# Graph network kernel on one core: neighbour counts moved into the later edge passes, and a first pass that takes stored and directly gathered tiles two and two

## The chip, the cores and the metric

The kernel runs on one core of a Trainium2 chip. The metric is the device time of one execution in microseconds (us). The engines are named as in the profile: PE (TensorE; PEld its weight loads), DVE (VectorE), ACT (ScalarE), POOL (GpSimd) and SP (SyncE). A "q" behind a name is that engine's instruction queue.

## The reference

There are 6250 nodes with 128 features and 106,250 directed edges, sorted by destination (`src`, `dst`). Four residual blocks follow each other, each with `x = layernorm(x + block(x))`:

- block 0, an attention layer: for each edge `s = leaky_relu(el[src] + er[dst])`, a softmax over the edges of one destination, and the weighted sum of the rows `(x @ W)[src]`;
- block 1, a message network: edge features (106,250 x 128) summed by source, then linear and softplus layers on the nodes;
- block 2, three attention layers of the same kind as block 0, with an edge term from three edge attributes, and batch norm in between;
- block 3, five layers `h + sum of h[src] over the edges of dst`, each followed by two linear layers and batch norms.

Block 3 needs, five times, the product of the features with the 6250 x 6250 matrix of edge counts ("how often does edge (i, j) occur"). This matrix is built once.

## The kernel before

**Tiles and steps.** Nodes lie in 49 blocks of 128 (`NB`). Edges lie in 208 tiles of 512 (`T`, `TE`; `W` = 4 columns of 128 edges). A tile whose edges end in two destination blocks is handled twice, so an edge pass has `K` = 256 steps for 208 tiles. The rows `(x @ W)[src]` are fetched by indirect DMAs of POOL from `gat_rows` in DRAM, 128 rows of 520 bytes each, four for a tile.

**The edge pass** `gat_edges` runs four times: once for block 0 (`streamed=True`), three times in a loop for block 2. In a later pass `fetch` gathers every tile into a `ring` of 16 tiles (L1204); SP waits until a slot is free and passes it on as `room`, and tells ACT over `tiles` which tiles have landed. `pipeline` writes the program of each engine by hand: 16 steps (`U`) in a loop body, before which the engine loads all registers of these steps. In a step, PE spreads the scores of step n (L1315), multiplies the weights of step n-7 with the ring's rows (L1324) and transposes the weights of step n-5 (L1331). DVE adds mask and scores (L1372), adds a product to the state (L1382), applies the slope (L1387), fetches scores (L1339), takes the maximum (L1345) and makes a mask (L1354). ACT adds a bias (L1402), loads a row for the mask by DMA (L1424), copies transposed weights out of PSUM (L1410), takes negatives (L1414) and the exponential (L1419). Four banks of PSUM hold spread scores, two the transposed weights, two the products.

**The streamed pass.** The gathered rows of block 0 don't depend on the stages before its pass. `gather_first_layer(begin, end)` is called by four earlier stages; POOL gathers tiles into five buffers (L1221) and stores each to `gathered` in DRAM itself (L1213). The pass then only loads them, by SP (L1240): 32 tiles are gathered in `positions`, 46 in `source_sums`, 12 in `adjacency_steps`, 118 in `adjacency`.

**The stages before the first pass**, each ended by a barrier of all engines (`end_phase`):

- `positions` finds for each edge its place in the order by source block. It runs over the source blocks twice in 26 chunks of 2048 edges, a count first, then comparison, scan, product and 32 small matmuls a chunk.
- `sort_rows` scatters the edge features to these places (POOL, L697) and counts rare edges.
- `source_sums` loads the sorted rows (SP, L1450) and sums them by source: comparison on DVE (L1483), matmuls (L1474), addition (L1494).
- `adjacency_steps` makes the tables for the count. The matrix is cut into 49 x 13 windows of 128 x 504 (`NKEY` = 637); a step adds the edges of one sorted tile to one window. POOL gathers twelve tables (L850).
- `adjacency` makes the counts in 1472 steps: DVE makes two tiles of ones and zeros (L1531, L1534), PE multiplies them into one of 8 banks (L1524), ACT copies pairs of windows out (L1568), clears the banks (L1570) and stores the pair (L1556).

The three functions of block 3 (`aggregate`, `second_layer`, `relu_norm`) read the matrix by SP (L1658).

## Time and profile before

| what | us |
|---|---|
| median of three runs | 8978.68 (8977.43 to 8986.32) |
| the profiled execution | 8993.16 |
| its span, first to last instruction | 8991.8 |
| mean granted clock of PE | 0.798 of full |
| busy: PE / DVE / ACT / POOL | 5567.6 / 4739.3 / 4511.6 / 4381.9 |

The profile is of one execution; its groups and windows below refer to its span. "Busy" adds up the durations of instructions, which on PE and ACT overlap a little; the distance between two starts is the better measure of what an instruction costs in a queue. The stages follow each other in time, so one reads a stage by giving the view its stretch: `positions` 177 to 487, `sort_rows` to 1552, `source_sums` to 1943, `adjacency_steps` to 2043, `adjacency` to 2746, the streamed pass 2770 to 3448, the later passes from 3690, 4840 and 5988, block 3 from 7170.

### The profile page before, as it was taken

Reading aid. Unit: us, or ns where it says so; the run is one execution under the profiler, and the core shown is the slowest. Engines: PE = TensorE matmul, PEld = TensorE weight load, DVE = VectorE, ACT = ScalarE, POOL = GpSimd, SP = SyncE. Lnnn points to the kernel's source line nnn. Section 1 sums busy time; section 2 is a strip of 40 time slices with the busy share of each in tenths; the row PEclk is TensorE's granted clock in tenths of the full one; section 3 lists DMA queues with packets and bytes.
Section 4 is the critical chain, followed back from the end, with each engine's and each line's share of the span. In section 5 each row is a group of like instructions: output and inputs, shape, how many; then the busy total and the mean of one; then the engine's idle time right before and its main releaser. Section 6 shows DMA issues by size and latency. Waiting matters only on the chain. (4 is left out here: it accounts for less than half of the span.)

```text
span 8991.8 us, 135316 instructions
## 1 busy us (share of the span) xinstructions
PE 5567.6 (62%) x30230; PEld 4477.6 (50%) x30231; DVE 4739.3 (53%) x12204; ACT 4511.6 (50%) x8872; POOL 4381.9 (49%) x4415
## 2 busy tenths in 40 slices
PE   1621111756776886466665666656666498998986
PEld 1610001742225774355554555645555487776865
DVE  3820000559997877555554555555555645445455
ACT  1038886008996774444444444444444444444344
POOL 1877777737771000477774777747777300000000
PEclk8555555878888998787886888778888799999998
DMA  3433334855665441233332333323333286676764
GB/s 102 120 101 105 107 105 111 233 136 183 211 211 160 135 131 46 65 84 85 84 84 70 85 84 84 85 69 84 84 84 84 57 264 199 217 251 199 252 212 154
DMA packets 724312, 1173.04 MB, mean 130 GB/s; under 512 B 118807, under 2 KB 546470, under 8 KB 723608
## 3 DMA queue, kind: packets, MB, share of 16 engines
q1 hardware_dynamic: 366644, 612.04, 22.0%
q0 software_dynamic: 150784, 336.22, 15.6%
q10 hardware_dynamic: 206628, 221.92, 8.7%
q8 instruction: 94, 1.54, 0.1%
q14 instruction: 162, 1.33, 0.0%
HBM read 955.51 MB, written 216.73 MB: 130 GB/s over the span
## 5 line engine op out<-in xcount | busy, mean ns | idle before, releaser
L1204 POOL DMA_INDIRECT ring<-gat_rows,src_idx x2496 | 2417.8, 969 | 1004.4 <-issue 1001.3
L1324 PE MATMUL ps<-ring,xT_b 128*128 x8192 | 1410.3, 325 | 1236.1 <-ACT xT_b L1410 1230.7
L1324 PEld LDWEIGHTS ps<-ring,xT_b 128*128 128x128 f32 x8192 | 1219.0, 228 | 1448.8 <-issue 1446.9
L1402 ACT ACTIVATE xT_a<-xT_a,state 128x514 f32<-128x514 f32 x1024 | 740.1, 723 | 1824.0 <-SPq L1176 1293.5
L1814 PE MATMUL ps<-wide,features 128*128 128x504 f32 (+1 forms) x6370 | 1438.8, 384 | 18.2 <-DVE features L1714 16.2
L1814 PEld LDWEIGHTS ps<-wide,features 128*128 128x128 f32 x6370 | 1156.8, 189 | 252.3 <-DVE wide L1682 17.4
L1372 DVE CUSTOM_DVE_ANT_0 xT_a<-ps,mask,xT_a 128x512 f32<-128x512 f32 x1024 | 767.0, 749 | 607.5 <-PE ps L1315 488.8
L697 POOL DMA_INDIRECT by_src<-ring,state x832 | 803.4, 966 | 255.9 <-issue 253.0
L1054 POOL TENSOR_TENSOR x_nodes<-x_nodes,last_state 128x1280 f32<-128x1280 f32 x3 | 9.9, 3312 | 1792.2 <-SPq L227 1792.2
L1315 PE MATMUL ps<-ident,s_col 128*128 128x128 f32 x4096 | 747.0, 315 | 187.5 <-DVE s_col L1339 122.5
L1419 ACT ACTIVATE xT_b<-xT_a,neg 128x514 f32<-128x514 f32 x1024 | 741.6, 724 | 33.1
L1331 PE MATMUL ps<-ident,xT_b 128*128 128x128 f32 x4096 | 751.8, 316 | 4.8 <-ACT xT_b L1419 4.8
L1387 DVE SCALAR_TENSOR_TENSOR xT_a<-xT_a 128x514 f32<-128x514 f32 x1024 | 704.1, 688 | 0.0
L1339 DVE TENSOR_TENSOR s_col<-ring,al_cols 128x4 f32 (+1 forms) x1036 | 166.5, 161 | 1019.5 <-ACTq L1400 980.5
L1680 DVE CAST wide<-xT_a 128x2016 fp32r<-128x2016 f16 (+27 forms) x440 | 410.8, 953 | 541.3 <-PE ps L1814 515.2
L1315 PEld LDWEIGHTS ps<-ident,s_col 128*128 128x128 f32 x4096 | 589.3, 164 | 211.3 <-DVE s_col L1339 128.0
L664 PE MATMUL ps<-xT_a 128*128 128x50 bf16 x832 | 184.4, 222 | 805.7 <-ACT xT_a L653 805.7
L1694 ACT ACTIVATE wide<-xT_a 128x1008 fp32r<-128x1008 f16 (+3 forms) x385 | 372.3, 978 | 605.0 <-PE ps L1814 594.2
L1221 POOL DMA_INDIRECT dl_all<-gat_rows,src_idx x484 | 571.5, 1181 | 147.6 <-issue 147.0
L1331 PEld LDWEIGHTS ps<-ident,xT_b 128*128 128x128 f32 x4096 | 598.9, 167 | 7.7 <-ACT xT_b L1419 7.7
L1410 ACT ACTIVATE xT_b<-ps 128x512 f32<-128x512 f32 x1024 | 595.6, 582 | 9.5 <-PE ps L1331 9.2
L664 PEld LDWEIGHTS ps<-xT_a 128*128 128x128 bf16 x832 | 87.1, 105 | 903.2 <-ACT xT_a L653 850.3
(383 smaller groups left out, 8761.4 us busy)
## 6 DMA issues: line engine op xcount, KB each, us to landing
xT_a<-adjacency SPq DMA_DIRECT2D x245, 756.0 KB
dl_all<-dloc_rows ACTq DMA_DIRECT2D x1052, 128.0 KB, 3.1
xT_b<-adjacency SPq DMA_DIRECT2D x150, 812.0 KB
xT_a<-adjacency SPq DMA_DIRECT2D x95, 812.0 KB
adjacency<-xT_b ACTq DMA_DIRECT2D x294, 252.0 KB
ring<-by_src SPq DMA_DIRECT2D x52, 1040.0 KB
ring<-gathered SPq DMA_DIRECT2D x208, 260.0 KB
ring<-in_edge_attr SPq DMA_DIRECT2D x103, 512.0 KB
```

What stands on the lines that cost most here:

```text
L697: pool.indirect_dma_start(by_src[:, :], bass.IndirectOffsetOnAxis(pos[:, g * L1U + u:g * L1U + u + 1], 0), ring[:, b * group + u * RC:b * ...
L1204: pool.indirect_dma_start(ring[:, o:o + RC], None, table[:, :], bass.IndirectOffsetOnAxis(src_idx[:, t * W + u:t * W + u + 1], 0)).then_in ...
L1221: pool.indirect_dma_start(held[h][:, u * RC:(u + 1) * RC], None, gat_rows[:, :], bass.IndirectOffsetOnAxis(src_idx[:, i:i + 1], 0)).then_i ...
L1315: m = pe.transpose(bank(BS + u % 4)[:, w * P:(w + 1) * P], s_col[u % 4][:, w:w + 1].to_broadcast([P, P]), ident[:, :])
L1324: m = pe.matmul(bank(BO + v % 2, R), pw[v % 4][:, w * P:(w + 1) * P], ring[:, w * RC:][:, bass.ds(look(SLOT, u - 7), R)], start=w == 0, st ...
L1331: m = pe.transpose(bank(BP + v % 2)[:, w * P:(w + 1) * P], pt[v % 8][:, w * P:(w + 1) * P], ident[:, :])
L1372: dve.tensor_tensor_reduce(out=m[:, 0:TE], in0=bank(BS + u % 4, TE), in1=mask[u % 4][:, :], scale=1.0, scalar=m[:, TE + 1:TE + 2], op0=ALU ...
L1387: dve.scalar_tensor_tensor(w, w, 0.2, w, ALU.mult, ALU.max).then_inc(q["leaky"], 1)
L1402: act.activation(um[u % 4], sm[u % 8], ACT.Identity, bias=S[:, ER:][:, bass.ds(look(BC, u), 1)]).then_inc(q["act_a"], 1)
L1410: act.activation(pw[v % 4], bank(BP + v % 2, TE), ACT.Copy).then_inc(q["pw_ready"], 1)
L1419: act.activation(pt[v % 8], um[v % 4], ACT.Exp, bias=neg[v % 4][:, :]).then_inc(q["weights"], 1)
L1814: m = pe.matmul(bank_of(w), H2[:, (i * 2 + x) * D:(i * 2 + x + 1) * D], wide[n % 2][:, o:o + width_of(w)], start=i == 0 and x == 0, stop=F ...
```

## The change

- **`adjacency` is gone.** Its counting is spread over the three later passes. The windows' steps are laid out for 2 streams x 3 passes x 256 steps = 1536. In each step of a later pass, for each of two streams, DVE makes the two tiles (`make_nodes`), PE multiplies the stream's last evicted window by the identity or by zeros (`carry`) and adds the new tile's product (`add_counts`), ACT copies the window out of PSUM (`evict_counts`) and in the next step stores it (`store_counts`): to its place in `counts` if the window ends there, to a row for waste otherwise. PE loads 16 registers each 8 steps, ACT 4 each 2 steps. Spread scores have two banks instead of four in these passes; the other two hold the two streams' windows. A window that both streams share is joined after the loop (four serial steps, three of them DMAs).
- **The tables** go to DRAM at the end of `adjacency_steps` (`of_steps`, `step_rows`) and each pass loads its third (`load_steps`).
- **The streamed pass** stores and loads tiles 0, 1, 4, 5, ... only. Tiles 2, 3, 6, 7, ... are gathered directly into the ring in the pass, by POOL.
- **The gathers before it:** 104 tiles instead of 208, in pairs with three buffers: 14 in `positions`, 72 in `source_sums`, 18 in `adjacency_steps`. The stores of the pairs are ACT's in the first and the last of these and SP's in `source_sums`, between its own loads.
- **`positions`** is written anew: one comparison of all 832 columns for each of 50 blocks, counts by PE, one scan, then for each block four matmuls and a maximum on DVE. The store of block numbers before it is gone (three DVE operations and two DMAs).

The diff, cut to its core:

```diff
-FIRST = 32
-EARLY = 78
-TABLES = 90
+FIRST = 14
+EARLY = 86
+STORED = T // 2
 RUN = 16
 NV = -(-(W * T) // RUN)
-NH = 5
-HELD = 3
+NH = 3
+PAIR = 2
...
+STREAMS = 2
+PASSES = 3
...
+PER = STREAMS * K
+DROP = NB * P * NWIN
...
+        counts = dram("counts", ((NB + 1) * P * NWIN, WD), F16)
+        adj = counts.rearrange("(i p w) c -> i p (w c)", p=P, w=NWIN)
+        of_steps = dram("of_steps", (2, P, AK))
+        step_rows = dram("step_rows", (2, AK), I32)
...
+            def count_bins():
+                for b in range(BINS):
+                    dve.tensor_scalar(hit[b], block, float(b), None, ALU.is_equal).then_inc(q["eq"], 1)
+                for b in range(BINS):
+                    pe.wait_ge(q["eq"], b + 1)
+                    for h in range(2):
+                        m = pe.matmul(PS[:, h * 512:h * 512 + HT], strip[:, 64 - b:192 - b],
+                                      hit[b][:, h * HT:(h + 1) * HT], start=b == 0, stop=b == BINS - 1)
                 m.then_inc(q["product"], 1)
...
+            def bin_starts():
+                dve.wait_ge(q["product"], 1)
+                s(dve, lambda: dve.tensor_copy(two(count), halves(0)))
+                s(dve, lambda: dve.tensor_tensor_scan(cum, count, count, 0.0, ALU.add, ALU.max))
...
+            def rank_bins():
+                s.wait(pe)
+                for b in range(BINS):
+                    if b >= 4:
+                        pe.wait_ge(q["summed"], b - 3)
+                    for h in range(2):
+                        to = PS[:, b % 4 * 1024 + h * 512:b % 4 * 1024 + h * 512 + HT]
+                        pe.matmul(to, earlier, hit[b][:, h * HT:(h + 1) * HT], start=True, stop=False)
+                        m = pe.matmul(to, choose[:, b:b + 1].to_broadcast([P, P]), pieces[:, h * HT:(h + 1) * HT],
+                                      start=False, stop=True)
+                    m.then_inc(q["masked"], 1)
+                for b in range(BINS):
+                    dve.wait_ge(q["masked"], b + 1)
+                    if b:
+                        dve.wait_ge(q["summed"], b)
+                    dve.tensor_tensor(two(best), two(best), halves(b % 4), ALU.max).then_inc(q["summed"], 1)
...
+            kept = gather_first_layer(0, FIRST)
+            for n in range(FIRST // PAIR):
+                keep_pair(act, 0, n)
+            end_phase(kept)
...
+            kept = gather_first_layer(EARLY, STORED)
+            for n in range((STORED - EARLY) // PAIR):
+                keep_pair(act, EARLY, n)
...
+            s.together(*[(sp, lambda c=c: sp.dma_start(of_steps[c, :, :], XTa[:, 3072 + c * AK:3072 + (c + 1) * AK]), 16)
+                         for c in range(2)], (dve, lambda: dve.tensor_copy(window_ids, node_ids[:, 0:WD])))
+            s.wait(sp)
...
+        def keep_pair(eng, begin, n):
+            h = n % NH
+            eng.wait_ge(q[f"rows{h}"], 16 * PAIR * W * (n // NH + 1))
+            eng.dma_start(gathered[begin // PAIR + n, :, :], held[h]).then_inc(q[f"kept{h}"], 16)
+
+        def first_tile(pair):
+            return pair * 2 * PAIR
+
+        def is_stored(g):
+            return g // PAIR % 2 == 0
...
                 for g in range(RT):
-                    if not first:
-                        sp.wait_ge(q["product"], free[g])
-                    sp.dma_start(ring[:, g * W * RC:(g + 1) * W * RC],
-                                 gathered[bass.ds(it * RT + g, 1), :, :].rearrange("a p c -> (a p) c")
-                                 ).then_inc(q[f"rows{g}"], 16)
-
-            load(0, True)
-            with sp.Fori(1, TITER) as it:
-                load(it, False)
-
-            with pool.Fori(0, TITER) as it:
-                for g in range(RT):
-                    pool.wait_ge(q[f"rows{g}"], it * 16 + 16)
-                    pool.sem_inc(q["tiles"], 1)
+                    if (not first or g >= RT - SOON) and (not last or g < RT - SOON):
+                        sp.wait_ge(q["product"], sp.snap(regs[g], min_val=1, max_val=K))
+                        later = (g + SOON) % RT
+                        if is_stored(later):
+                            load(it + (g + SOON) // RT, later)
+                        else:
+                            sp.sem_inc(q["room"], 1)
+                    if is_stored(g):
+                        sp.wait_ge(q[f"rows{g}"], it * 16 + 16)
+                    else:
+                        sp.wait_ge(q[f"got{g}"], it * (16 * W) + 16 * W)
+                    sp.sem_inc(q["tiles"], 1)
...
+            for n in range(T - STORED):
+                turn, i = divmod(n, len(direct))
+                g = direct[i]
+                if turn:
+                    pool.wait_ge(q["room"], n - len(direct) + 1)
+                for u in range(W):
+                    o = (g * W + u) * RC
+                    at = (turn * RT + g) * W + u
+                    pool.indirect_dma_start(ring[:, o:o + RC], None, gat_rows[:, :],
+                                            bass.IndirectOffsetOnAxis(src_idx[:, at:at + 1], 0)
+                                            ).then_inc(q[f"got{g}"], 16)
...
+            wide_scores = 4 if streamed else 2
+            spread = lambda u: bank(BS + u % wide_scores)
+            tile = lambda x: bank(2 + x, WD)
...
+            def rows_of(eng, used, count, tab, n, top):
+
+                regs = step_regs[eng.engine][used:used + count]
+                eng.load(regs, tab[0:1, bass.ds(n * STREAMS, count)])
+                return [eng.snap(r, min_val=0, max_val=top) for r in regs]
...
+            def make_nodes(n, u, have):
+
+                if have(2):
+                    dve.wait_ge(q["added"], n * STREAMS - STREAMS)
+                dve.tensor_tensor(node1[u % 4].rearrange("p (x n) -> p x n", n=P), node_row,
+                                  src_steps[:, u * STREAMS:][:, bass.ds((n - u) * STREAMS, STREAMS)]
+                                  .rearrange("p (x a) -> p x a", a=1).to_broadcast([P, STREAMS, P]), ALU.is_equal)
+                for x in range(STREAMS):
+                    m = dve.tensor_scalar(node2[u % 2 * STREAMS + x], window_ids,
+                                          dst_steps[:, u * STREAMS + x:][:, bass.ds((n - u) * STREAMS, 1)],
+                                          None, ALU.is_equal)
+                m.then_inc(q["eq"], 1)
+
+            def add_counts(n, u, have):
+
+                pe.wait_ge(q["eq"], n + 1)
+                if have(1):
+                    pe.wait_ge(q["out"], n * STREAMS)
+                if u % 8 == 0:
+                    keep_at[:] = rows_of(pe, 2 * U, 8 * STREAMS, keep_tab, n, P)
+                for x in range(STREAMS):
+                    pe.matmul(tile(x), carry[:, bass.ds(keep_at[u % 8 * STREAMS + x], P)], evicted[(u - 1) % 2 * STREAMS + x],
+                              start=True, stop=False)
+                    pe.matmul(tile(x), node1[u % 4][:, x * P:(x + 1) * P], node2[u % 2 * STREAMS + x],
+                              start=False, stop=True).then_inc(q["added"], 1)
+
+            def evict_counts(n, u, have):
+
+                for x in range(STREAMS):
+                    act.wait_ge(q["added"], n * STREAMS + x + 1)
+                    if have(2):
+                        act.wait_ge(q[f"st{u % 2 * STREAMS + x}"], (n - u) * 8 + u // 2 * 16)
+                    act.activation(evicted[u % 2 * STREAMS + x], tile(x), ACT.Copy).then_inc(q["out"], 1)
+
+            def store_counts(n, u, later):
+
+                for x in range(STREAMS):
+                    act.wait_ge(q["out"], n * STREAMS + x + 1)
+                    act.dma_start(counts[bass.ds(store_at[later % 2 * STREAMS + x], P, step=NWIN), :],
+                                  evicted[u % 2 * STREAMS + x]).then_inc(q[f"st{u % 2 * STREAMS + x}"], 16)
...
+                if have(0) and not streamed:
+                    add_counts(n, u, have)
...
+                    if not streamed:
+                        make_nodes(n + 1, (u + 1) % U, lambda d: have(d - 1))
...
+                if not streamed and u % 2 == 0 and (have(0) or have(1)):
+                    store_at[:] = rows_of(act, 2 * U, 2 * STREAMS, at_tab, n, DROP + NWIN - 1)
+                if have(1) and not streamed:
+                    store_counts(n - 1, (u - 1) % U, u)
+                if have(0) and not streamed:
+                    evict_counts(n, u, have)
...
+            loads, pairs = T // RG, (EARLY - FIRST) // PAIR
+            kept_now = 0
+            for g in range(RG, loads):
+                sp.load(seen, fr[0:1, g:g + 1])
+                load(g, g % RG, sp.snap(seen[0], min_val=1, max_val=K2))
+                while kept_now < pairs and (kept_now + 1) * (loads - RG - 4) <= (g - RG - 2) * pairs:
+                    keep_pair(sp, FIRST, kept_now)
+                    kept_now += 1
+            for n in range(kept_now, pairs):
+                keep_pair(sp, FIRST, n)
...
         adjacency_steps()
-        adjacency()
...
+            gat_edges(l * KW + KW, turn=l)
...
+        s(sp, lambda: sp.dma_start(part, where), 16)
+        s(dve, lambda: dve.scalar_tensor_tensor(part, evicted[STREAMS], share, part, ALU.mult, ALU.add))
+        s(sp, lambda: sp.dma_start(where, part), 16)
...
```

## Rows read from the trace of the kernel before

**Rows 1.** Windows by stage: us, busy PE, PEld, DVE, ACT, POOL, clock, DMA, GB/s

```profile
178.00:488.00 310.00, 182.23 (x834) 179.91 (x834) 234.84 (x124) 34.94 (x42) 267.37 (x162) 0.50 0.47 124
...
1556.00:1945.00 389.00, 281.07 (x2048) 275.13 (x2048) 233.77 (x516) 18.29 (x104) 218.14 (x232) 0.86 0.76 205
...
2048.00:2745.00 697.00, 495.87 (x1472) 155.71 (x1472) 644.62 (x1838) 628.03 (x638) 551.05 (x590) 0.87 0.66 208
```

**Rows 2.** Timeline at the adjacency's edges: start, us, engine, line

```profile
2043.46 3.47 DVE L1517 MEMSET ps<- 128x4096 f32 x1 [1.74 <-PEq L227]
...
2747.59 1.37 ACT L891 ACTIVATE rows<-state 128x640 f32 x2 [13.52 <-PEq L886]
```

**Rows 3.** Windows of the streamed pass and of the last later pass

```profile
2770.00:3448.00 678.00, 545.38 (x4096) 489.79 (x4096) 537.93 (x1800) 522.89 (x1024) 0.00 (x0) 0.94 0.46 133
5988.00:7072.00 1084.00, 658.24 (x4096) 595.84 (x4096) 569.37 (x1798) 518.30 (x1025) 806.22 (x832) 0.81 0.38 83
```

**Rows 4.** One line's instructions, L1204 in the last later pass

```profile
L1204 POOL DMA_INDIRECT ring<-gat_rows,src_idx x832: 940/944/1456, 5988.6 to 7047.1; - x167
```

**Rows 5.** Timeline of the adjacency stage, PE and DVE

```profile
2599.84 4.06 PE L1524 MATMUL ps<-ring,xT_a 128*128 128x504 bf16 x10
...
2601.29 1.29 DVE L1534 TENSOR_SCALAR ring<-xT_b,xT_a 128x504 bf16<-128x504 int16 x4
```

**Rows 6.** Timeline of one step of the streamed pass

```profile
3000.88 1.15 PE L1324 MATMUL ps<-ring,xT_b 128*128 x8 [0.36 <-ACT xT_b L1410]
...
3001.64 0.73 ACT L1402 ACTIVATE xT_a<-xT_a,state 128x514 f32<-128x514 f32 x1
3001.68 0.69 DVE L1387 SCALAR_TENSOR_TENSOR xT_a<-xT_a 128x514 f32<-128x514 f32 x1
...
3002.28 0.58 ACT L1410 ACTIVATE xT_b<-ps 128x512 f32<-128x512 f32 x1
3002.29 0.15 DVE L1339 TENSOR_TENSOR s_col<-ring,al_cols 128x4 f32 x1
...
3002.49 0.34 DVE L1354 TENSOR_SCALAR mask<-dl_all,iota_p 128x512 bf16<-128x512 bf16 x1
...
3002.98 0.72 ACT L1419 ACTIVATE xT_b<-xT_a,neg 128x514 f32<-128x514 f32 x1
```

**Rows 7.** Window of the source sums while POOL gathers

```profile
1556.00:1830.00 274.00, 196.98 (x1428) 192.91 (x1429) 164.21 (x359) 13.72 (x78) 217.03 (x230) 0.85 0.88 240
```

**Rows 8.** Window of the adjacency stage, POOL's gathers of L1221 alone

```profile
2043.00:2745.00 702.00, 485.45 (x472) 0.86 0.65 207
```

**Rows 9.** Timeline of the adjacency's steps, SP's store and POOL's first table gather

```profile
1998.35 0.39 SPq L846 DMA_DIRECT2D sorted_ids<-xT_a  x1
...
2011.92 1.00 POOL L850 DMA_INDIRECT xT_a<-sorted_ids,xT_b  x1 [0.30 <-issue]
```

**Rows 10.** Timeline of a later pass beside the gathers

```profile
4206.22 2.08 PE L1324 MATMUL ps<-ring,xT_b 128*128 x8 [2.18 <-ACT xT_b L1410]
...
4210.01 0.53 DVE L1354 TENSOR_SCALAR mask<-dl_all,iota_p 128x512 bf16<-128x512 bf16 x1
```

**Rows 11.** Timeline of ACT in the adjacency stage, a register load before 2668.01

```profile
2664.53 1.01 ACT L1570 ACTIVATE ps<-xT_b 128x1008 f32<-128x1008 f16 x1
...
2665.48 0.99 ACT L1568 ACTIVATE xT_b<-ps 128x1008 f16<-128x1008 f32 x1
2666.50 1.01 ACT L1570 ACTIVATE ps<-xT_b 128x1008 f32<-128x1008 f16 x1
2666.51 0.33 ACTq L1556 DMA_DIRECT2D adjacency<-xT_b  x1
2668.01 1.01 ACT L1568 ACTIVATE xT_b<-ps 128x1008 f16<-128x1008 f32 x1 [0.49 <-PE ps L1524]
```

**Rows 12.** Timeline of DVE at the turn of 16 steps

```profile
3358.68 0.75 DVE L1372 CUSTOM_DVE_ANT_0 xT_a<-ps,mask,xT_a 128x512 f32<-128x512 f32 x1 [4.37 <-PE ps L1315]
```

**Rows 13.** One line's DMAs, L1424 in a later pass

```profile
DMA to landing us min/median/max: 2.9/3.0/4.0
```

429 lines of the change are left out of this document (189 added, 240 removed).

## Prediction

> **What bounds the kernel now.** I read the windows by stage first, then the groups of instructions, then short stretches of the timeline. The chain of waits ends in the last normalization and says nothing of the stages changed here. Every stage ends in a barrier of all engines, so times add up stage by stage.
>
> [rows 1] positions (178 to 488): POOL 267 us busy, DVE 235, TensorE's clock at its lower level. Source sums (1556 to 1945): PE 281, DVE 234, POOL 218, DMA share 0.76. Adjacency (2048 to 2745): DVE 645 and ACT 628 of 697, POOL 551. [rows 2] give the adjacency's edges: its memset starts at 2043.46, the next stage's first ACTIVATE at 2747.59.
>
> [rows 3] the first edge pass (streamed) and a later one, both 256 steps: 678 us with no POOL work, 1084 with it; PE, DVE and ACT do equal work in both. [rows 4] POOL issues 832 gathers between 5988.6 and 7047.1: 1.274 us each, four to a tile, 5.10 a tile, with 208 tiles to 256 steps, so 4.14 us a step. Its queue never stops. A later pass is thus bound by POOL's gathers; the streamed pass shows what the other engines need, 678/256 = 2.65 a step with both ends in it, so 1.5 us a step is free.
>
> **The change, part by part** (profiled execution: span 8991.8 us, 8993.16 in all; the median of the three runs is 14.5 lower and I take that off at the end).
>
> *Adjacency stage gone.* The steps' stage is now followed directly by the turn of nodes to features: 2747.6 − 43.5 − about 2 for a barrier that the step stage keeps anyway, so 702 us [rows 2]. What it did goes to the later passes (counting) and elsewhere (its 118 tiles' gathers). **−702**.
>
> *Positions.* Two passes over 26 chunks with scan and product go. New: 50 DVE comparisons of 832 columns, 100 matmuls of 416 columns that run beside them, a serial start (scan and a dozen small steps), 200 matmuls, 50 DVE maxima of 832 from PSUM. A 504-column comparison recurs every 0.30 us (four in 1.29) [rows 5], so 832 take 0.47 and all 24. A 504-column bf16 matmul at the lower clock recurs in 0.41 (ten in 4.06) [rows 5], 416 columns 0.34: 34 us for the counts, 68 for the ranks. A two-input operation on 514 columns recurs in 0.61 (3001.68 to 3002.29) [rows 6], 832 take 0.98, with the wait for its predecessor 1.1: 55 for the ranks, beside PE's 68 (34 at the higher clock; the 0.50 of [rows 1] stands over products of two columns and says little). 34 + 14 + 64 + 8 is 120 against 309: **−189** (−160 to −205). POOL has 14 tiles to gather, 70 us at the pace of [rows 4], hidden; the 7 stores by ScalarE end under the ranks.
>
> *Before it:* three DVE operations and two stores of block numbers go, serial: **−6**.
>
> *Source sums.* POOL now gathers 72 tiles, not 46: 288 × (1.03 + 0.30) is 383 us; the stage takes 389 [rows 1]. (1.03 is a gather beside a busy DVE, [rows 8], 485.45/472; 0.30 is what the pace of [rows 4] has above the mean 806.22/832 = 0.97 of [rows 3].) SP stores 36 pairs between its own loads: load g+1 is queued behind a pair whose gathers must land, and POOL waits for a buffer that SP gives back. So SP's loads fall to POOL's pace, 383 plus the last loads' landing and use, some 25. DMA moves 79 MB now, 92 then, and the stretch with gathers already has share 0.88 [rows 7]. I take 408: **+20** (0 to +60).
>
> *Steps of the adjacency.* The twelve POOL gathers of the step tables stand behind the tiles' gathers in POOL's queue: they start at 2011.9 while their input was stored from 1998.35 on [rows 9]. Eighteen tiles instead of twelve end 18 × 5.1 = 92 us after 1944 (their stores are ScalarE's now), against 67: +25; the added one-partition operations (1536 elements, about 1.6 us each) run before that and are hidden. Storing the two tables of 786 KB adds 5, the iotas 2: **+32** (+20 to +45).
>
> *Streamed pass.* Half its tiles come by gathers: 416 × 1.27 is 530 us of POOL in a pass of 678, two tiles in four, with 16 slots of ring: hidden, but 78% of the cover is used. The start waits for tile 3, the second direct one: 2 × 5.1 + 2 instead of 9, so +4; the mask operation, 0.34 here [rows 6], takes up to 0.53 beside gathers [rows 10]; a quarter of that difference on average is +0.04 × 256 = 11. **+15** (0 to +60; a loss of cover would show as waits for tiles).
>
> *Later passes, three times.* Each step gets: DVE a 256-column comparison and two of 504, 0.33 + 0.60; PE four matmuls of 504, 1.64 at the lower clock [rows 5], half of it, 0.84 with gaps, at the higher; ACT two evictions of 504 from PSUM, 0.47 each (1008 recur in 0.95 to 1.03 [rows 11]) and two stores, 0.33 of its queue each [rows 11], and every second step a load of four registers. That load shows in [rows 11]: the eviction follows at 1.51 instead of 0.95, of which the sequencer's share after the DMA issue is 1.18. ACT's step is now 0.64 (bias) + 0.70 (weights out, neg) + exp [rows 6]. New: exp's 0.66 covers part of the queue's work, which is 2 × (0.33 + 0.09 for the address) = 0.84 in one step and 1.95 with the load in the other; then 0.95 for the evictions. 3.13 and 4.24, mean 3.7.
>
> To this comes the turn of each 16 steps: DVE loads 48 registers, and its next step starts after 4.37 us of idle time [rows 12], with PE's load 5.6 a turn or so, 0.35 of the 2.65 a step. PE's new load of 16 registers each 8 steps holds the counts back by 1 us or so: 0.1. Sum **4.15 a step**, beside 4.14 for the gathers: neither bound is clear of the other. DVE has 538/256 = 2.1 of work [rows 3] + 0.93 + 0.35 = 3.4, PE 545/256 = 2.1 + 0.84 + 0.3 = 3.3.
>
> The pass is then 256 × 4.2 + the first four tiles (20) + the drain of eight steps (8) = 1103. Queued behind ACT's new wait for the counts are the next step's bias operation, and with it DVE's next slope and PE's weights; nothing of theirs is late while PE finishes its counts within ACT's 3 us. The wait for the store two steps back: a 128 KB transfer on this queue lands in 2.9 to 4.0 [rows 13], the buffer is wanted one step (4.2) later. The stores are 512 × 129 KB = 66 MB in a pass, 60 GB/s beside today's 83 [rows 3], where [rows 7] show 240. Just hidden; without cover 0.5 us a step. Two rates so close disturb each other: I add 15. 1118 against 1083: **+105** for three (below: +8 each, the longer drain alone; above: +250 each, if PE stays at the lower clock for most of a pass).
>
> The page "SBUF — State Buffer" of the Trainium skill (Who interferes with whom) says that a DVE operation in a two-port mode and a GpSimd operation lock each other out for a whole instruction. Whole instructions aren't lost here: beside the adjacency's DVE, 92% busy with just these comparisons [rows 1], a gather took 1.03 [rows 8], in the passes 0.97 [rows 3]. Three more such operations a step are a quarter of that stage's density: +0.017 × 832 is 14 us a pass, inside my 15. By the rule each of the three would hold up a gather for its length, 0.9 us a step, 230 a pass (rival E).
>
> *Rest.* Table loads at a pass's start run beside the first gathers; setting carry +1 a pass; joining the two streams at the end, four serial transfers of 2 to 3 us: **+13**. The adjacency's layout that the last stages read is the same.
>
> Sum: −702 − 189 − 6 + 20 + 32 + 15 + 105 + 13 = −712. 8993.2 − 712 − 14.5 = **8267**.
>
> **Rivals.** *A, the gathers stay the bound.* The register loads hide more than I give them, a step costs 3.9 or less, the passes take +12 each: 8267 − 69 = **8198**. For it: streamed, ACT and DVE reach 2.3 between turns. Against: ACT within a tenth of the bound by the sum above. Chance 0.27.
> *B, ACT and PE hold each other.* PE falls to the lower clock after a wait for a tile (a group of eight takes 2.08 at 4206 [rows 10], 1.15 at 3001 [rows 6]); its step is then 2.1 × 1.8 + 1.64 = 5.4, ACT's evictions wait, and a step costs 4.6 on average: 28 + 1178 = 1206, +123 a pass, 8267 − 105 + 369 = **8530**. For it: granted clock 0.81 in the passes, 0.94 streamed [rows 3]. Against: the clock is high where PE is busiest, and the counts fill PE's idle time. Chance 0.25.
> *C, slower than before.* PE at the lower level throughout, its step 5.4 and the turns: 256 × 5.6 + 28 = 1462, +379 a pass; everything else saves 817: 8978.7 − 817 + 1137 = **9299**. It decides from +272 a pass, 5.2 us a step. Against: 0.81 already with PE waiting 40% of a pass [rows 3]. Chance 0.03, with all else that ends slower.
> *D, the covered POOL work comes out:* source sums and streamed pass both POOL- or DMA-bound, +60 and +60 instead of +35: **8350**. Chance 0.1.
> *E, the new comparisons hold up POOL.* Each of three a step stops the running gather for its own 0.3 us; POOL's queue, which never stops in a pass, gets 230 us longer, not 15: 8267 + 3 × 215 = **8910**. Against: 1.03 beside a DVE at 92% [rows 8]. Chance 0.03.
> Forecast 0.32.
>
> **How the numbers follow.** The range reaches from A with a cheaper positions stage (8140) to B with some of D (8560); left out are about 0.13 above (C, E, part of B) and 0.07 below. Faster by over 0.2% in all cases but C: 0.96, same 0.01, slower 0.03; 0.2% is about what a measurement of this kernel tells from no change.
>
> **What would show it.** No instruction between the steps' stage and the next turn: −702. Positions under 130 us, else the ranks cost more. The later passes: 1.27 to 1.30 a gather with few waits on a "room" semaphore means A; POOL waiting for room and ACT with under 10% of idle time means ACT bounds; ACT waiting for PE's counts and a granted clock under 0.85, B. Passes outside 1090 to 1210 make the prediction wrong.

## The result, and the profile after

The changed kernel takes **8270.24 us** (median of 4 runs, 8267.22 to 8274.54) beside 8978.78 for the kernel before (4 runs); the ratio is 0.921 with a 95% interval of 0.9194 to 0.9226. Forecast was 8267. The profiled execution has a span of 8265.9 us, 725.9 less than that of before.

The stages again follow each other, so the difference can be read stage by stage. First the windows of the changed kernel (columns as in [rows 1]): positions, source sums, steps of the adjacency, first pass, and the three later passes.

```profile
172.00:261.00 89.00, 64.56 (x302) 27.29 (x302) 77.55 (x122) 0.19 (x2) 55.04 (x58) 0.92 0.30 85
1328.60:1759.40 430.80, 300.17 (x2048) 293.77 (x2048) 233.95 (x513) 18.28 (x104) 300.96 (x289) 0.81 0.81 218
1759.40:1899.00 139.60, 13.04 (x43) 8.53 (x43) 45.68 (x73) 0.17 (x1) 92.48 (x87) 0.51 0.32 98
1922.40:2604.00 681.60, 546.99 (x4096) 490.06 (x4096) 538.77 (x1798) 522.37 (x1024) 413.72 (x416) 0.94 0.51 132
2847.00:3969.00 1122.00, 789.43 (x5120) 597.88 (x5120) 777.85 (x2572) 772.27 (x1537) 826.10 (x832) 0.91 0.60 141
4036.00:5156.00 1120.00, 781.69 (x5120) 590.69 (x5120) 778.58 (x2569) 772.23 (x1537) 823.62 (x832) 0.92 0.61 141
5224.00:6345.00 1121.00, 789.25 (x5120) 595.00 (x5120) 777.49 (x2572) 772.61 (x1537) 823.57 (x832) 0.92 0.60 141
```

Against [rows 1, 3]: positions has become short and PE's clock in it high; source sums are longer with more DMA; the first pass now has 414 us of POOL work in it and is hardly longer; the later passes have 200 us more DVE work, 250 more ACT work, and a granted clock of 0.91 to 0.92 instead of 0.81. DMA share 0.60 instead of 0.38 is the stores of counts.

| stage | before | after | difference | forecast |
|---|---|---|---|---|
| up to positions | 177.3 | 172.1 | -5.3 | -6 |
| positions | 309.4 | 88.8 | -220.6 | -189 |
| sort_rows | 1067.7 | 1067.8 | 0 | 0 |
| source sums | 388.9 | 430.8 | +41.9 | +20 |
| steps of the adjacency | 100.1 | 139.5 | +39.4 | +32 |
| adjacency | 704.1 | gone | -704.1 | -702 |
| turn of the nodes, first pass | 699.2 | 704.6 | +5.4 | +15 |
| three later passes, to the last state update | 3624.9 | 3740.6 | +115.7 | +105 |
| after that | 1920.1 | 1921.8 | +1.7 | +13, elsewhere too |
| **span** | 8991.8 | 8265.9 | **-725.9** | **-712** |

(A pass's last update of the state is at L1382 before and at L1515 after. The row of the later passes begins with the first pass's last update; 244 us of it are the layer norm and products between the first pass and the next, which did not change.)

Now `positions` by groups of instructions (line, engine, op, count | busy us, mean ns | idle before), the four that matter:

```profile
L601 DVE TENSOR_TENSOR state<-state,ps 128x832 f32<-128x832 f32 x50 | 51.0, 1021 | 7.3 <-PE ps L594 2.4
L594 PE MATMUL ps<-state,al_cols 128*128 128x416 f16 x100 | 35.2, 352 | 0.0
...
L593 PE MATMUL ps<-ring,al_cols 128*128 128x416 bf16 x40 | 13.8, 344 | 5.0 <-DVE state L601 5.0
...
L555 DVE TENSOR_SCALAR ring<-al_cols 128x832 bf16<-128x832 bf16 x20 | 6.5, 402 | 0.0
```

The maxima (L601) fill 51 of the 57 us of the ranks, and PE waits for them (last row but one): the ranks are bound by DVE, at 1.14 us each, not by PE. The head of the steps' stage:

```profile
1758.26 0.29 DVE L1646 TENSOR_TENSOR state<-state,ps 128x128 f32 x1 [0.20 <-DVE state L1646]
1759.36 0.14 POOL L804 IOTA xT_b<- 128x12 f32 x1 [18.27 <-DMA gathered<-rows_mask]
1759.68 8.53 POOL L808 IOTA ring<- 1x768 f32 x2 [0.19 <-POOL xT_b L804]
1768.25 0.58 DVE L815 CAST xT_a<-src_cols 1x831 int32<-1x831 f32 x1 [9.70 <-POOL ring L808]
1768.39 1.27 POOL L1259 DMA_INDIRECT gat_stage<-gat_rows,src_idx  x1 [0.17 <-issue]
```

Two one-partition iotas take 8.5 us, and both DVE's chain and POOL's 72 gathers begin behind them.

A later pass is measured best by two rows of one line each (count: shortest/median/longest ns, first to last start). The second later pass, before (L1204 gathers, L1382 updates) and after (L1233, L1515):

```profile
L1204 POOL DMA_INDIRECT ring<-gat_rows,src_idx x832: 940/944/1471, 4838.0 to 5897.2; - x167
L1382 DVE SCALAR_TENSOR_TENSOR state<-state,xT_b,ps x256: 338/346/351, 4891.1 to 5921.1; 128x129 f32 x128
```

```profile
L1233 POOL DMA_INDIRECT ring<-gat_rows,src_idx x832: 940/944/1462, 4036.0 to 5112.0; - x167
L1515 DVE SCALAR_TENSOR_TENSOR state<-state,xT_b,ps x256: 338/346/351, 4091.7 to 5155.3; 128x129 f32 x128
```

Before, the gathers take 1059 us from first to last (1.275 each) and the state's last update starts 24 us behind the last gather: 1083. After, they take 1076 (1.295) and the tail is 43: 1119. So the +36 of this pass are 17 of slower gathers and 19 of a longer tail. (The first and the third later pass went from 1081 to 1120 and from 1083 to 1119.) The median gather is the same 944 ns; some gathers are longer. And POOL waited for nobody, while three engines waited for each other (the first later pass, 2850 to 3900; engine, what it was about to do <- what it waited for: us, times, longest):

```profile
POOL ring L1233 <- issue: 246.6, 809, 0.3
...
ACT al_cols L1429 <- issue: 161.1, 216, 1.7
ACT xT_a L1537 <- DVE xT_a L1505: 96.7, 28, 6.8
...
DVE xT_a L1505 <- issue: 244.7, 195, 8.3
...
PE ps L1418 <- ACT al_cols L1429: 176.7, 181, 3.0
```

"Issue" before ACT's eviction is its own queue (DMA issues and register loads). PE's counts wait for that eviction. This looks as if two things bind at once, POOL's gathers and ACT's queue; the experiments take them apart.

### The profile page after: what moved, and what is told of

Read it like the earlier page. It is cut to its first block and busy times, and to the rows that moved or that the text cites. A ratio compares the mean times of both kernels' runs of the same rounds, so it can differ in the third digit from the quotient of the medians.

```text
span 8265.9 us, 141750 instructions
## 1 busy us (share of the span) xinstructions
PE 5352.1 (65%) x31293; PEld 4178.9 (51%) x31294; DVE 4566.5 (55%) x12677; ACT 4612.0 (56%) x9736; POOL 4195.4 (51%) x4209
## 5 line engine op out<-in xcount | busy, mean ns | idle before, releaser
L1233 POOL DMA_INDIRECT ring<-gat_rows,src_idx x2496 | 2473.3, 991 | 1044.3 <-issue 1043.1
L1453 PE MATMUL ps<-ring,xT_b 128*128 x8192 | 1202.7, 293 | 260.1 <-ACT xT_b L1545 247.4
L1505 DVE CUSTOM_DVE_ANT_0 xT_a<-ps,rows_mask,xT_a 128x512 f32<-128x512 f32 x1024 | 768.4, 750 | 1014.4 <-issue 760.0
L1453 PEld LDWEIGHTS ps<-ring,xT_b 128*128 128x128 f32 x8192 | 1081.2, 205 | 328.7 <-issue 327.1
L1429 ACT ACTIVATE al_cols<-ps 128x504 f16<-128x504 f32 x1536 | 823.2, 588 | 590.2 <-issue 517.3
L1418 PE MATMUL ps<-al_cols,w_static 128*128 128x504 f16 x1536 | 622.4, 405 | 697.4 <-ACT al_cols L1429 561.9
L1444 PE MATMUL ps<-ident,s_col 128*128 128x128 f32 x4096 | 659.6, 287 | 204.4 <-issue 108.1
L1444 PEld LDWEIGHTS ps<-ident,s_col 128*128 128x128 f32 x4096 | 529.7, 146 | 390.0 <-issue 170.2
L1460 PE MATMUL ps<-ident,xT_b 128*128 128x128 f32 x4096 | 659.2, 287 | 0.0
L1418 PEld LDWEIGHTS ps<-al_cols,w_static 128*128 x1536 | 154.4, 101 | 973.9 <-issue 895.4
L1420 PE MATMUL ps<-gat_stage,w_static 128*128 128x504 bf16 x1536 | 618.3, 403 | 0.0
```

The source lines that it names most:

```text
L1233: pool.indirect_dma_start(ring[:, o:o + RC], None, table[:, :], bass.IndirectOffsetOnAxis(src_idx[:, t * W + u:t * W + u + 1], 0)).then_in ...
L1418: pe.matmul(tile(x), carry[:, bass.ds(keep_at[u % 8 * STREAMS + x], P)], evicted[(u - 1) % 2 * STREAMS + x], start=True, stop=False)
L1429: act.activation(evicted[u % 2 * STREAMS + x], tile(x), ACT.Copy).then_inc(q["out"], 1)
L1444: m = pe.transpose(spread(u)[:, w * P:(w + 1) * P], s_col[u % 4][:, w:w + 1].to_broadcast([P, P]), ident[:, :])
L1453: m = pe.matmul(bank(BO + v % 2, R), pw[v % 4][:, w * P:(w + 1) * P], ring[:, w * RC:][:, bass.ds(look(SLOT, u - 7), R)], start=w == 0, st ...
L1460: m = pe.transpose(bank(BP + v % 2)[:, w * P:(w + 1) * P], pt[v % 8][:, w * P:(w + 1) * P], ident[:, :])
```

## The experiments

"Pass" is always first gather to the last state update of the second later pass, from two rows like the ones above, and "period" the gathers' mean distance. The expectations count a pass in another way, to the first gather of the next pass: 1188 in the changed kernel, 1148 to 1151 before, some 68 us more than in the table below. Where the counts are not stored to their places, the table of counts would hold nothing, so these kernels fill it with zeros in a stage of its own (about 200 us, outside all stages compared).

**No counting at all.** `make_nodes`, `add_counts`, `evict_counts`, `store_counts` and ACT's `rows_of` are not called.

```diff
-                if have(0) and not streamed:
-                    add_counts(n, u, have)
...
-                if not streamed and u % 2 == 0 and (have(0) or have(1)):
-                    store_at[:] = rows_of(act, ...)
```

> The changed kernel without any counting in the three later passes: no comparisons, no count products, no evictions, no stores, no register loads for them (the tables are still loaded); a stage of its own ahead of the adjacency's steps fills the count table with zeros, and its time is taken off. In the changed kernel a pass from its first gather to the next pass's first takes 1188.5 us, before it took 1149; the gathers recur in 1.296 us (1.274 before) and the last state update comes 42 us after the last gather (23 before). Theory (counting alone costs this, in two parts of about 20 each): gathers back to 1.274, the tail back to 23, a pass 1149 to 1151. Rival (something else of the change slows the passes, as the table loads or where the data lie): a pass stays over 1160.

**Comparisons alone.** As above, but `make_nodes` stays, without its wait for PE.

```diff
-                if have(2):
-                    dve.wait_ge(q["added"], n * STREAMS - STREAMS)
```

> Of the counting in the later passes only VectorE's three comparisons a step are left; products, evictions, stores and register loads are left out, and the same stage fills the table with zeros. Theory: the +0.022 us of a gather (18 us a pass) comes from VectorE's comparisons beside GpSimd, so the gathers stay at 1.290 to 1.300, while the tail falls to 23 to 25 us: 1168 to 1172 a pass. Rival 1 (the stores' traffic of 66 MB a pass slows the gathers): 1.274 and 23, 1150 a pass. Rival 2 (GpSimd waits for room in the ring, seen as long gathers, since ScalarE is behind): 1.274 too, as ScalarE has nothing more to do.

**Everything but the stores** and ACT's waits for them.

```diff
-                if have(1) and not streamed:
-                    store_counts(n - 1, (u - 1) % U, u)
```

> The counting is complete but for the stores: no DMA of counts and no wait for one, the register loads of their addresses stay; the table is filled with zeros in a stage of its own. Theory (comparisons slow the gathers, ScalarE's queue makes the tail): gathers stay at 1.29, the tail falls from 42 to about 25 to 30, since ScalarE issues two DMAs of 0.33 less in a step: 1172 to 1178 a pass. Rival 1 (traffic slows the gathers): 1.275 and a tail of 25 to 30, 1155 to 1160. If neither number moves (1188), the stores are free.

**Stores to fixed places**, so no register loads by ACT for them.

```diff
-                    store_at[:] = rows_of(act, 2 * U, 2 * STREAMS, at_tab, n, DROP + NWIN - 1)
...
-                    act.dma_start(counts[bass.ds(store_at[later % 2 * STREAMS + x], P, step=NWIN), :],
+                    act.dma_start(counts[bass.ds((u % 2 * STREAMS + x) * P * NWIN, P, step=NWIN), :],
```

> The counting with its stores, but at four fixed places, so that ScalarE loads no registers for their addresses; the table is filled with zeros in a stage of its own. Theory (ScalarE's queue with the register load in every second step sets the step): the steps no longer alternate between 3.45 and 4.0 us but take 3.4 or less, sixteen of them 67 instead of 68.3, the tail 23 to 27, gathers still 1.295: a pass 1170 to 1175. Rival (the turn of each sixteen steps makes the tail, the load is hidden): 68.3 and 42 stay, 1186 to 1190. My working gave the load some 1.1 us every second step; if it is not hidden and ScalarE were the only bound, 16 steps would fall by 9.

These four ran together (beside them the kernel before took 8972). The rows, one pair each for no counting, comparisons alone, no stores, fixed places:

```profile
L1233 POOL DMA_INDIRECT ring<-gat_rows,src_idx x832: 940/944/1469, 4195.8 to 5251.0; - x167
L1511 DVE SCALAR_TENSOR_TENSOR state<-state,xT_b,ps x256: 336/346/352, 4248.6 to 5274.6; 128x129 f32 x128
```

```profile
L1233 POOL DMA_INDIRECT ring<-gat_rows,src_idx x832: 940/945/1448, 4242.1 to 5338.8; - x167
L1511 DVE SCALAR_TENSOR_TENSOR state<-state,xT_b,ps x256: 338/347/369, 4294.4 to 5363.2; 128x129 f32 x128
```

```profile
L1233 POOL DMA_INDIRECT ring<-gat_rows,src_idx x832: 940/945/1458, 4238.6 to 5333.1; - x167
L1513 DVE SCALAR_TENSOR_TENSOR state<-state,xT_b,ps x256: 336/346/353, 4292.5 to 5358.9; 128x129 f32 x128
```

```profile
L1233 POOL DMA_INDIRECT ring<-gat_rows,src_idx x832: 940/945/1480, 4240.8 to 5333.7; - x167
L1515 DVE SCALAR_TENSOR_TENSOR state<-state,xT_b,ps x256: 338/347/355, 4295.2 to 5361.7; 128x129 f32 x128
```

| second later pass | gathers, us | period | tail | pass |
|---|---|---|---|---|
| kernel before | 1059 | 1.275 | 24 | 1083 |
| no counting | 1055 | 1.270 | 24 | 1079 |
| comparisons alone | 1097 | 1.320 | 24 | 1121 |
| all but stores | 1095 | 1.317 | 26 | 1120 |
| stores to fixed places | 1093 | 1.315 | 28 | 1121 |
| the changed kernel | 1076 | 1.295 | 43 | 1119 |

Counting costs 40 us a pass, and **the comparisons alone cost all of it** (1121 against 1079; each kernel was profiled once, and its three later passes lie within 1077 to 1079 and 1120 to 1123): with them POOL's gathers need 1.320 us each. My expectation that they would stay at 1.290 to 1.300 and that a pass would take 1168 to 1172 (measured 1188 in the same count) was wrong, and so were both rivals, traffic and room: with no store and no wait for room the gathers are slowest. Taking the stores or the register loads from ACT shortens the tail to 26 to 28, about as expected, but not the pass: the gathers then take back what the tail gives. With fixed places the steps between two turns lie mostly at 3.3 to 3.6 us instead of 3.45 and 4.03 in turn, but sixteen steps with their turn still take 68.4 (67 expected). So ACT's queue is what makes the tail of 43, and freeing it gains nothing while the comparisons hold up POOL. The two limits lie at the same 1120.

A gather that is held up shows in its own duration. Of the 832 in this pass, 50 are longer than 1.1 us in the kernel before, 40 with no counting, 169 with comparisons alone, 155 without stores, 141 with fixed places and 80 in the changed kernel, and the period follows this count. Why fewer are held up (1.295) exactly when ACT is late, I can only argue: DVE then works in other places of POOL's cycle.

**Which comparison?** Comparisons alone, with the two of 504 columns only (`tensor_tensor` of 256 columns left out), and the reverse.

```diff
-                dve.tensor_tensor(node1[u % 4].rearrange("p (x n) -> p x n", n=P), node_row,
...
```

```diff
-                for x in range(STREAMS):
-                    m = dve.tensor_scalar(node2[u % 2 * STREAMS + x], window_ids,
...
```

> As the kernel with comparisons alone, but of the three a step only the two of 504 columns are left (the one of 256 columns with two operands is left out too). Comparisons alone made 167 of 832 gathers longer than 1.1 us (40 without any) and the gathers' period 1.320 for 1.269: +42 us a pass. Theory (each comparison of 16-bit values in SBUF holds up the gather that it meets, by its own length): 0.60 of 1.02 us of comparisons a step are left, so +25 of the +42: a period of 1.299, 110 to 120 long gathers, a pass of 1170. Rival 1 (it is the operation with two operands that collides): 1.275, 1150 a pass. Rival 2 (any work that fills VectorE's gap behind the mask does it): 1.31 to 1.32 remain, 1185.

> The kernel with only the two comparisons of 504 columns (no counting otherwise, nor the comparison of 256 columns), again, since the kernel before took 10,598 us beside its first run, and GpSimd waited there for transfers. Without comparisons the gathers' period was 1.269 and a pass 1145 us, with all three 1.320 and 1188. Theory (each comparison holds up the gather that it meets by its length): 1.299, 1170 a pass. Rival 1 (the operation with two operands collides): 1.275, 1150. Rival 2 (any filling of VectorE's gap does it): 1.31 to 1.32, 1185.

> As the kernel with comparisons alone, but only the one comparison of 256 columns with two operands (0.42 us a step) is left, the two of 504 columns (0.60 together, one operand and a scalar for each partition) are left out. So far: none 1.269 a gather and 1145 us a pass; the two of 504 alone 1.313 and 1184; all three 1.320 and 1188. Theory (the form with one operand and a scalar collides with GpSimd, the one with two operands does not): 1.269 to 1.280, 1145 to 1155 a pass. Rival (any filling of VectorE's gap does it, and the first half us saturates it): 1.300 to 1.315, 1172 to 1184. By length alone it would be 1.290, 1163.

The first and the last of these runs can't be compared with the others: they ran on two other chips, on which the kernel before took 10,598 and 10,380 us. POOL then waited for room in the ring (202 us in this pass of the last one), the period was 1.53 and 1.49, and neither says anything about comparisons. Only the second counts (beside it the kernel before took 8995, beside the four above 8972):

```profile
L1233 POOL DMA_INDIRECT ring<-gat_rows,src_idx x832: 938/944/1484, 4239.7 to 5330.6; - x167
L1508 DVE SCALAR_TENSOR_TENSOR state<-state,xT_b,ps x256: 336/343/352, 4293.2 to 5355.2; 128x129 f32 x128
```

A period of 1.313 and a pass of 1115.5: the two of 504 alone already cost 36 of the 42 us, and the one of 256 adds 6. (The third later pass took 1119.6, as long as with all three; so the 6 is within what passes of one kernel differ by.) Proportion to length (25 of 42) is refuted. It stays open whether the form with one operand is what collides or whether the first half microsecond does, whatever it is; the run that would have told was one of the two that can't be compared.

**Comparisons elsewhere in the step**: ahead of the slope instead of behind the mask.

```diff
+                if have(0) and not streamed:
+                    make_nodes(n + 1, (u + 1) % U, lambda d: have(d - 1))
                 if have(1):
                     w = um[(u - 1) % 4]
...
                     make_mask(n + 2, u + 2)
-                    if not streamed:
-                        make_nodes(n + 1, (u + 1) % U, lambda d: have(d - 1))
```

> The changed kernel with VectorE's three comparisons moved ahead of the slope, behind the state's update, so that the run of SBUF work behind the slope is broken up (directly behind the masked maximum there were not enough registers). Theory (unbroken runs collide most): period 1.28 for 1.296 of the gathers, the slope comes up to 1 us later, a pass 1180 to 1200. Rival 1 (the comparisons' total counts): 1.296 and 1188 stay. Rival 2 (the later slope rules): 70 us or more for sixteen steps, 1210 or more a pass, 8330 in all.

```profile
L1233 POOL DMA_INDIRECT ring<-gat_rows,src_idx x832: 940/944/1730, 4033.6 to 5100.4; - x167
L1515 DVE SCALAR_TENSOR_TENSOR state<-state,xT_b,ps x256: 343/347/351, 4087.1 to 5148.6; 128x129 f32 x128
```

Period 1.284, tail 48, pass 1115; in all 8252.28 (2 runs), ratio 0.9175 (0.9158 to 0.9192) to a kernel before of 8994.85. The same instructions in another place make the gathers 0.011 us shorter: place matters, as the first theory said, but the tail takes half of it. This pass gained least. Over all three later passes `order` takes 1108, 1115 and 1113 us with periods of 1.283 to 1.285; the three kernels that leave the comparisons behind the mask (the changed one and the two below, `small_again` and `both`) take 1116 to 1121 in all nine passes, with 1.287 to 1.298. That is some 7 us a pass, or 21 in all, beside 18 in the medians. The ratio's interval ends just where that of the changed kernel begins, so by the times alone the gain is barely clear.

**Small moves ahead of the first pass.** Memsets on DVE for POOL's iotas, and SP stores its first pairs three loads earlier. The first text stands ahead of the run on a slow chip (`y_small`), the second ahead of its repetition.

```diff
-            s.together(*[(pool, lambda x=x: pool.iota(drop[...], ...)) for x in range(STREAMS)])
+            s.together(*[(dve, lambda x=x, j=j: dve.memset(drop[:, x * AK // 2 + j:(x + 1) * AK // 2:2],
+                float(DROP + 2 * x + j))) for x in range(STREAMS) for j in range(2)])
...
-                while kept_now < pairs and (kept_now + 1) * (loads - RG - 4) <= (g - RG - 2) * pairs:
+                while kept_now < pairs and (kept_now + 1) * (loads - RG - 4) <= (g - RG + 1) * pairs:
```

> The changed kernel, with two small moves: the two iotas on GpSimd at the head of the adjacency's steps (8.5 us on the path) become four short memsets on VectorE, and in the source sums SyncE stores its first pairs about three loads earlier, since GpSimd stood 23.6 us waiting for its first buffer. Theory (source sums are bound by GpSimd's pace plus this stall, the iotas are serial): adjacency's steps 139.5 to 131 to 133, source sums 430.8 to 409 to 413: about 8243 in all. Rival (in source sums SyncE's loads are the bound, the stall is absorbed and comes back at the last load): source sums stay within 5 us of 431, 8262.

> The changed kernel with the iotas as memsets and the earlier first stores, again for the same reason. Theory: adjacency's steps 131 to 133 (139.5 in the changed kernel), source sums 409 to 413 (430.8), 8243 in all. Rival (SyncE's loads are the bound of the source sums): 426 to 431, 8262.

The first run stood beside a kernel before of 10,598 again (10,011.11). The second took 8275.03 (2 runs), ratio 0.92 (0.9183 to 0.9217): no measurable gain. Its windows of source sums and steps:

```profile
1329.90:1762.90 433.00, 290.91 (x2048) 282.81 (x2048) 231.89 (x513) 18.27 (x104) 301.47 (x289) 0.84 0.81 217
1762.90:1894.80 131.90, 13.06 (x44) 8.56 (x44) 47.19 (x77) 0.81 (x2) 83.61 (x84) 0.50 0.35 103
```

The steps' stage is 7.7 shorter, as expected. Source sums stay at 433: the stall of 23.6 us of POOL is gone (its last gather comes 20 us earlier, and it then idles 41 us), but the sums end no sooner. They are bound by SP's queue, where a load waits behind a pair's store for nearly the whole stage, and by their own work after the last loads; the rival was right. The end of SP's queue shows it, first in the changed kernel, then here:

```profile
1742.65 0.35 SPq L1240 DMA_DIRECT2D gathered<-rows_mask  x1
1743.44 0.36 SPq L1596 DMA_DIRECT2D ring<-by_src  x1
```

```profile
1723.04 0.35 SPq L1239 DMA_DIRECT2D gathered<-rows_mask  x1
1723.85 9.68 SPq L1595 DMA_DIRECT2D ring<-by_src  x4
```

The last store is 20 us earlier, but four loads are left behind it where one was left before.

**Fewer tiles stored ahead**: three pairs in eight instead of every second, 78 tiles for 104 (14, 52 and 12 in the three stages), 130 gathered directly in the first pass. `both` has the small moves too.

```diff
-STORED = T // 2
+STORED = T * 3 // 8
+KEPT_OF = (0, 3, 6)
...
-            return g // PAIR % 2 == 0
+            return g // PAIR % (RT // PAIR) in KEPT_OF
...
-EARLY = 86
+EARLY = 66
```

> The changed kernel with 78 tiles stored ahead instead of 104 (three pairs of eight instead of every second): 52 of them in source sums (72 before), 12 in the adjacency's steps (18 before), and 130 tiles gathered directly in the first pass (104 before). Theory: source sums are bound by GpSimd and fall to what the sums need, 389 to 395 (430.8 now); adjacency's steps fall by 6 tiles of 5.2 us to 108 to 112; the first pass has 520 gathers of 1.28, 666 us plus a start of 10 under the 681 it takes, so it goes up by 5 to 20: in all -50 to -65, 8205 to 8220. Rival (cover used up: beside VectorE a gather takes 1.30 to 1.32 and the ring runs dry at each turn): the first pass 710 to 720, in all -35, 8235.

> Both in one: the memsets and earlier stores, and 78 tiles stored ahead instead of 104. On the slow chip the second of these alone took 45 us less than the first alone: source sums -81, adjacency's steps -21, first pass +55. Theory here: source sums 388 to 395, adjacency's steps 105 to 112, the first pass +5 to +25 over 681: 8270 - 38 - 31 + 15 = 8216, 8200 to 8230; ratio to the kernel before 0.915. Rival (the first pass is bound by its gathers, +40 or more): 8240 to 8250, no better than the small moves alone.

On the chip where the kernel before took 10,598, the share alone took 9966.41 and the small moves alone 10,011.11. On the faster one `both` took **8245.75** (5 runs, 8231.35 to 8251.95), ratio 0.9167 with an interval of 0.9155 to 0.918, clear of the changed kernel's 0.9194 to 0.9226. That is 29 us less than the small moves alone, but not clear of `order` (0.9158 to 0.9192); the two were not put together. Expected were 8200 to 8230. Source sums, steps and first pass:

```profile
1330.30:1740.00 409.70, 283.97 (x2048) 278.04 (x2048) 232.75 (x513) 18.29 (x104) 219.88 (x209) 0.85 0.74 203
1740.00:1840.60 100.60, 11.75 (x44) 7.41 (x44) 47.40 (x77) 0.80 (x2) 61.33 (x60) 0.53 0.34 104
1863.90:2571.20 707.30, 548.55 (x4096) 491.60 (x4096) 542.18 (x1798) 521.62 (x1024) 518.08 (x520) 0.93 0.54 127
```

Against the changed kernel: source sums -21 (expected -36 to -43), steps -39 with the memsets' 8 (-27 to -34), first pass +26 (+5 to +25). The total came out where the rival had it (8240 to 8250), though not for its reason, a first pass longer by 40 or more: the source sums gave about half of what was expected, and the first pass took a little more. The first pass is now bound by its gathers: POOL waits for room 13 us in it, where in the changed kernel it waits 127:

```profile
L1310 POOL DMA_INDIRECT ring<-gat_rows,src_idx x520 | 518.1, 996 | 211.5 <-issue 198.1 <-SPq L1287 13.1 <-DMA ring<-gat_rows,src_idx 0.3
```

```profile
L1311 POOL DMA_INDIRECT ring<-gat_rows,src_idx x416 | 413.7, 995 | 282.5 <-issue 155.1 <-SPq L1288 127.1 <-DMA ring<-gat_rows,src_idx 0.3
```

## Why the prediction was right, step by step

*Adjacency stage gone* (-702, measured -704; the 43.5 in its sum stands for 2043.5) and *before positions* (-6, -5.3): right.

*Positions* (-189, measured -221): the largest miss, and outside the term's own range of -160 to -205. The comparisons of 832 columns recur in 0.32 us, not in 0.47 scaled up from 504. PE had its high clock (0.92 granted, where [rows 1] show 0.50 before), so the counts end 22 us after the start, not 34. And the ranks are DVE's 57 us, not PE's 64 (the rows that the prediction shows make it 68). The serial part took 9, not 14. I had written the high clock down only as a bound.

*Source sums* (+20, measured +42): the mechanism, SP's loads falling to POOL's pace, was right; the number left out the way SP's order ties both. With 26 pairs instead of 36 the stage still takes 21 us more than before, and removing POOL's stall gave nothing. *Steps of the adjacency* (+32, +39): the gathers 25 as forecast (26.5 measured: 94.4 us from the first to the tables' first, 67.9 before), the iotas 8.5 instead of 2, confirmed by the memsets.

*First pass* (+15, +5): the direct gathers are hidden, with POOL waiting 127 us for room. `both` shows the edge of that cover: 25% more gathers cost 26 us.

*Later passes* (1118 each, measured 1119 to 1121): right in size, and "neither bound is clear of the other" was right in a stronger sense than I meant. The step chain: ACT's evictions start 3.45 and 4.02 us apart between turns,

```profile
3899.87 1.07 ACT L1429 ACTIVATE al_cols<-ps 128x504 f16<-128x504 f32 x2 [1.33 <-issue]
...
3903.32 1.07 ACT L1429 ACTIVATE al_cols<-ps 128x504 f16<-128x504 f32 x2 [0.44 <-issue]
...
3907.34 1.07 ACT L1429 ACTIVATE al_cols<-ps 128x504 f16<-128x504 f32 x2 [1.01 <-issue]
```

and over the pass the updates of the state mostly alternate between 3.45 and 4.03: a mean of 3.74, forecast 3.7. Sixteen of them take 68.2 with the turn and PE's loads of 16 registers, so these cost 8.4, forecast 7.2: 4.26 a step, forecast 4.15. The other bound, the gathers, I had mis-sized: 14 us a pass for the added comparisons, measured 42 when they are alone. Both errors go the same way and each sets a pass of 1120, and the 15 us that I had added for "two rates so close" covered them. That was a guess which fitted, not a mechanism.

*Rivals.* A needed gathers undisturbed; they were not, and the passes took +36 to +40 each. The sign that the prediction named for A, 1.27 to 1.30 a gather with few waits for room, did come (1.295 and none): it can't tell A from the forecast, since ACT fell behind without ever filling the ring, and its lateness shows in the tail alone. B fell: the granted clock rose to 0.91 to 0.92, because the counts fill PE's idle time (0.80 without them in the run of comparisons alone). E had the right mechanism at a fifth of its size: +42 against 230. D asked for +60 and +60 in source sums and first pass; they came out at +42 and +5.

*What the prediction had wrong about the gathers* is the step "whole instructions aren't lost here". It was read from a mean (1.03 us beside the adjacency's DVE), and a mean can't show it: of those 472 gathers, 93 took 1.1 to 1.5 us, on average 0.29 more than the usual 0.944. The experiments say the same. 0.73 us of one-operand comparisons a step lengthen 3.25 gathers by 0.14 us together (1.313 against 1.270), a fifth of the comparisons' length. But this is not spread evenly: 134 gathers of that pass are longer than 1.1 us where 40 are without comparisons, by 0.39 us on average, about one comparison (0.36). All 134 started while DVE was in the slope operation, ahead of the comparisons; of the 132 that started during a comparison none was long. The page "SBUF — State Buffer" of the Trainium skill (Who interferes with whom) says that a VectorE operation in a two-port mode and a GpSimd operation exclude each other for the whole instruction. The counts fit a loss of a whole comparison that comes only when it meets a certain part of a gather; no run here shows which mode these comparisons run in, or what in the gather is held up.

*The rest* (+13, measured +5, of which 3 between the passes), and the median: I took off the 14.5 us by which the profiled execution of before was slower than its median; the profiled one of after is 3 faster than its own. That error of 17 and the -14 of the sum cancel. Inside the sum the misses cancel too: by the rows of the table, -32 in positions, -10 in the first pass and -11 in the last row stand against +22, +7 and +11. So the agreement within 3 us is luck. What the trace bears out is the large terms, above all the stage that went, and each other term within 32 us.

## What to carry to other kernels

Of each instruction that is added beside an engine that bounds a stage, ask what it does to that engine's own instructions: here VectorE had almost a third of the pass free and still set the whole price. Count the instructions that are held up one by one; a mean hides them. Where two engines bound a stage at the same level, relieving one shows nothing in the time, so read the gathers' period and the tail apart. Read every pass, not one: passes of one kernel differ by up to 9 us here (1114 to 1123 with fixed places). Cover is used up at a point that can be worked out (104 tiles in the first pass cost 5 us, 130 cost 31), and going past it pays only if the work costs more where it is now (60 us).

## What the runs showed of the hardware

- A gather issued by GpSimd takes 944 or 945 ns in the median in every later pass shown, and 1.1 to 1.7 us when it is held up beside VectorE: 40 of 832 without comparisons, 134 with 0.73 us of one-operand 16-bit comparisons a step, which cost 36 us a pass. Moving all three comparisons within the step gives back 0.011 of the 0.025 us that a gather had lost in the full kernel, at the price of a longer tail.
- An iota of 768 elements on one partition takes 4.3 us on GpSimd (8.53 for two); four strided memsets in their place on VectorE, 1.6 us together, took 7.7 us off the stage.
- The kernel before took 8972 and 8995 us on two chips and 10,380 and 10,598 on two others, there with a granted clock of 0.75 instead of 0.80. In the other kernels that ran on the two slow chips GpSimd waited some 200 to 340 us a pass for room in the ring, while the time behind the last pass (block 3, without gathers) was 1921 to 1923 us, and 1920 to 1923 on the others. What makes these chips slow was not looked for.
